# Splitting the generator's projection weights during the expert tiles and keeping the halves in DRAM

## The chip, the cores and the metric

The kernel is one program that runs on one core of a Trainium2 chip. Its time is device microseconds from start to end of the program, as a median of several executions. One further execution was taken with the hardware profiler; its trace is what the sections below read.

## What is computed

A two-layer decoder on x (32 sequences of 128 tokens, 256 features, written B, S and D in the kernel). Six stages follow each other, each adding to x. The two that matter here are the third and the fourth:

```python
# third stage: for each token the two best of 8 experts, weights by softmax of the two scores
u, v = x @ W1[e], x @ W2[e]
h = u * sigmoid(u) * v
out += (h @ W3[e]) * weights[..., e]
# fourth stage, on the normalized x
h_mean = mean(x, axis=1)                                  # one vector of 256 for each sequence
params = h_mean @ omega_proj_w.T + omega_proj_b           # 2016 numbers: the upper triangle of 64 x 64
omega = triangle(params) - triangle(params).T
G = I + omega + omega@omega/2 + omega@omega@omega/6
lie_out = (x[:, :, :64] @ G) @ omega_out_w.T + omega_out_b
out = rmsnorm(x + omega_mix * lie_out + vq_mix * vq_contribution, norm_w)
```

The weights of `params` (omega_proj_w) are the generator's projection weights. The host lays them out as a full 64 x 64 square for each of 256 features: 8192 f32 values on each of 128 partitions, 4 MB in all. The kernel multiplies with f16 pairs: a value times a power of two is kept as its f16 rounding (the high half) and the f16 of what is left (the low half), and a product is the sum of three f16 products.

## The kernel before, in words

**Order of the whole.** `decoder` calls six stage functions. Within one, each engine has its own instruction list, and semaphores order them; a block ends when every engine has reached its end. `give_back` then clears the stage's semaphores.

**The expert tiles (`expert_tiles`, from line 876).** The routing part before it sorts 2 x 4096 token choices into 39 tiles of 256 rows. For each tile GpSimd gathers the rows with two indirect DMAs (`gather`, L907, four tiles ahead) and scatters the results (`scatter`, L915). TensorE goes through: first half of the hidden columns (`up(n, 0)`), the rest of the tile before (`down(n-1, 1)`), the transposes of the next tile, `up(n, 1)`, `down(n, 0)`. ScalarE's and VectorE's lists are written out by hand in `step`: ScalarE does sigmoid, high half of h, result copy, high half of the next input, sigmoid, high half of h; VectorE does the gate (two operations), low half of h (L1038), low half of the next input (L1024), the gate again and the low half again. SyncE has nothing to do in this block.

**The generator stage (`lie_rotation`, from line 1689), its front.** SyncE issues, in this order, the 16 loads of expert results (eight groups of four sequences, two results for each token, 512 KB each), with the four quarters of the projection weights (`Wp`, 1 MB each, L1776) between them, then the constants and small weights, then the held weights of the next stage. VectorE adds the results to X (`add`, L2025: eight instructions to a group), takes statistics of two groups at a time (`stats`), GpSimd takes the root (`invert`, L1961), VectorE makes the shift (`negate`, L2049), ScalarE writes the normalized rows (`norm`, L1898), TensorE transposes the first 64 features (L1799) and sums the rows for the mean (L1803), ScalarE and VectorE keep the transposed rows as halves (`high` L1903, `low` L2055). VectorE's list is: add(2h), negate(h-1), add(2h+1), low(2h-2), stats(h), low(2h-1), for h = 1, 2, 3.

**The split before the change.** In ScalarE's list, `omega_piece` stands after the groups 2 and 3 (two quarters) and again after the groups 4 and 5 (two quarters); each is two activations over 2048 columns, one that scales `Wp` by 16 in place (L1908) and one that writes the high half (L1910). GpSimd's `omega_low` (L1966) makes the low half from the scaled weights and the high half: two quarters after `invert(2)`, two after `invert(3)`.

**What waits for it.** TensorE's `omega` (L1812: 64 rows of the square, six matmuls each, in seven runs with the code book's matmuls between them) waits for the four low quarters and for the mean's halves. `Wp` is afterwards used as scratch for the small results and for omega, which is why VectorE also waits for the low quarters ahead of the scratch's first use, and SyncE ahead of `shift_rows`.

Of the kernel before, what the change touches and what calls it, by code (L numbers as in the profile page):

```python
# [5 lines left out]
f16 = mybir.dt.float16  # L6
# [8 lines left out]
P = 128  # L15
# [552 lines left out]
def moe_swiglu(nc, sems, X, ident, power, A, ahead):  # L568

    SCALE = 256.0  # L570
    HID = HIDDEN
    HC = HID // P
    with ExitStack() as scope:
        c = Core(nc, scope, sems, "m_")
        owner = c.sb("owner", [P, TILES], i32)
        fetch, deliver = c.sb("fetch", [P, BLOCKS], u32), c.sb("deliver", [P, BLOCKS], u32)
        W1, W2 = ([c.sb(f"w{n}{t}", [P, E, DC, HID], f16) for t in range(2)] for n in (1, 2))
        W3 = [c.sb(f"w3{t}", [P, E, HC, D], f16) for t in range(2)]
        weights = [(A["split_w"][i, t], flat(w[t][:])) for i, w in enumerate((W1, W2, W3)) for t in range(2)]
        with ExitStack() as routing:  # L580
            dispatch(nc, Core(nc, routing, sems, "mr_"), X, ident, power, A, ahead, SCALE, weights, owner, fetch,
                     deliver)
        with ExitStack() as tiles:
            expert_tiles(nc, Core(nc, tiles, sems, "mt_"), ahead.area, ident, W1, W2, W3, SCALE, HC, owner, fetch,
                         deliver, A["token_rows"], A["expert_results"])

# [289 lines left out]
def expert_tiles(nc, c, area, ident, W1, W2, W3, SCALE, HC, owner, fetch, deliver, rows,  # L876
                 results):

# [18 lines left out]


    with nc.Block() as block:  # L899
        @block.gpsimd  # L900
        def _(pool):
# [78 lines left out]
        def _(act):  # L980
# [18 lines left out]
            def result(n, k, p, old):  # L999
# [3 lines left out]
                act.activation(yout[p][:, :, :], pY[:, :, :], ACT.Copy, scale=1.0 / SCALE).then_inc(y_copied, 1)  # L1003

            def step(n, k, p, age):
                sigmoid(n, 0, age == 0)
                hidden_high(n, 0, age == 0)
                if age > 0:
                    result(n - 1, k - 1 + p, 1 - p, not starts(n, 1) and not starts(n, 2))
                if not starts(n, TILES - 1):  # L1010
                    high(n + 1, 1 - p, age > 0)
                sigmoid(n, 1, age == 0)
                hidden_high(n, 1, age == 0)
            nc.scalar.preload_act_table(ACT.Sigmoid)
            high(0, 0, False)
            for n in range(TILES):
                step(n, n // 2, n % 2, min(n, 2))
            result(TILES - 1, (TILES - 1) // 2, 0, True)

        @block.vector  # L1020
        def _(dve):
# [19 lines left out]
            def step(n, k, p, age):  # L1041
# [4 lines left out]
                gate(n, 1, age == 0)  # L1046
                hidden_low(n, 1)
            low(0, 0)
            for n in range(TILES):
                step(n, n // 2, n % 2, min(n, 2))  # L1050


# [636 lines left out]
def lie_rotation(nc, sems, X, ident, power, A, ahead):  # L1689
# [5 lines left out]
    with ExitStack() as scope:  # L1695
# [24 lines left out]
        for n, rows, width in (("vq", B, LD), ("vsq", B, LD), ("csq", CODES, LD), ("bo2", B, D), ("vnorm", B, LD), ("cnorm", CODES, LD), ("vT", LD, B),  # L1720
# [35 lines left out]
            "consts_in w_in wp_in ones added1 added2 stat summed scaled ve rstd shifted xn turned high low meant kept "  # L1756
            "hm_high hm_low wp_scaled wp_high wp_low half_made norms step vq_projected vnorm cnorm both_turned turned_kept "
            "scores hot hot_turned hotT code_taken vqo vqo_turned vqoT vq_out shift16 shift_rows woo_mixed woo_high woo_low "
# [3 lines left out]
        def each(b0, n):  # L1762
            return slice(b0, b0 + n)

        with nc.Block() as block:
            @block.sync
            def _(sp):
                results = A["expert_results"][0:2 * B * S, :].rearrange("(k p b) d -> k p b d", k=2, b=B)
                piece = 0
                for g in range(NG):  # L1770
                    at = each(g * GB, GB)
                    sp.dma_start(XN[:, at, :], results[0][:, at, :]).then_inc(in1[g], 16)
                    sp.dma_start(R2[:, at, :], results[1][:, at, :]).then_inc(in2[g], 16)
                    if g in (1, 3, 4, 5):
                        columns = each(piece * WIDE, WIDE)
                        sp.dma_start(Wp[:, columns], flat(A["L1_attn_Wp"])[:, columns]).then_inc(s["wp_in"], 16)  # L1776
                        piece += 1
                sp.dma_start(mix[:, 0:1], A["L1_attn_omega_mix"].partition_broadcast(P)).then_inc(s["consts_in"], 16)
# [5 lines left out]
                for t, n in ((bvi, "L1_attn_vq_proj_in_b"), (bvo, "L1_attn_vq_proj_out_b"), (boo, "L1_attn_omega_out_b")):  # L1784
                    sp.dma_start(t[:, :], A[n].partition_broadcast(B)).then_inc(s["w_in"], 16)
                ahead.load(sp, "mqa")
                sp.wait_ge(s["shift16"], 2)
                sp.wait_ge(s["wp_low"], 4)
                for t in range(2):
# [3 lines left out]
            def _(pe):  # L1793
# [57 lines left out]
                last.then_inc(s["vq_projected"], 1)  # L1851
                pe.wait_ge(s["wp_low"], 4)
                pe.wait_ge(s["hm_low"], 1)
# [40 lines left out]
            def _(act):  # L1894
# [9 lines left out]

                def omega_piece(n):
                    columns = each(n * WIDE, WIDE)
                    act.wait_ge(s["wp_in"], 16 * 4)
                    act.activation(Wp[:, columns], Wp[:, columns], ACT.Copy, scale=PSCALE).then_inc(s["wp_scaled"], 1)  # L1908
                    act.wait_ge(s["wp_scaled"], n + 1)
                    act.activation(flat(Wp16[0][:])[:, columns], Wp[:, columns], ACT.Copy).then_inc(s["wp_high"], 1)  # L1910

                def G_high(h):
# [19 lines left out]
                for g in range(0, NG, 2):  # L1932
# [3 lines left out]
                    high(g + 1)  # L1936
                    if g == 2:
                        omega_piece(0)
                        omega_piece(1)
                    if g == 4:  # L1940
                        omega_piece(2)
                        omega_piece(3)
                act.wait_ge(s["meant"], 1)
# [13 lines left out]
            def _(pool):  # L1957
# [4 lines left out]

                def omega_low(n):
                    columns = each(n * WIDE, WIDE)
                    pool.wait_ge(s["wp_high"], n + 1)
                    pool.tensor_tensor(flat(Wp16[1][:])[:, columns], Wp[:, columns], flat(Wp16[0][:])[:, columns],  # L1966
                                       ALU.subtract).then_inc(s["wp_low"], 1)

                def root(g):
# [17 lines left out]
                invert(2)  # L1987
                omega_low(0)
                omega_low(1)
                invert(3)  # L1990
                omega_low(2)
                omega_low(3)
                pool.wait_ge(s["half_made"], 1)
# [11 lines left out]
            def _(dve):  # L2005
# [115 lines left out]
                for h in range(1, NG // 2):  # L2121
# [16 lines left out]
                   .then_inc(s["hm_low"], 1)  # L2138
                dve.wait_ge(s["wp_low"], 4)
                step(dve.tensor_scalar(v["bo2"][:, :], boo[:, :], mix[0:B, 0:1], None, ALU.mult))  # L2140
# [1033 lines left out]
def decoder(nc, A, out, stages):  # L3174
    with ExitStack() as whole:
# [15 lines left out]
        A["ctx_parts"] = nc.dram_tensor("ctx_parts", (2, NG, P, DC * GT), f16, kind="Internal").ap()  # L3191
        A["shares"] = nc.dram_tensor("shares", (NG // 2, 2 * GB * E, P), f32, kind="Internal").ap()
        A["m_bounce"] = nc.dram_tensor("m_bounce", (2, 2, D, GT), f16, kind="Internal").ap()
        ahead = Ahead(c, A, stages)
# [100 lines left out]
```

## Time and profile before

| | |
|---|---|
| median of three executions | 1752.41 us (1751.7 to 1754.59) |
| the profiled execution | 1740.78 us |
| its span, first to last instruction | 1739.1 us |
| TensorE busy over the span | 1300.8 us (75%) |
| VectorE, ScalarE, GpSimd busy | 62%, 47%, 43% |
| HBM read, written | 102.34 MB, 48.10 MB |

Spans and starts are counted from the first instruction. The stages lie at about 0 to 238 (attention), 238 to 579 (retention), 579 to 1015 (experts: routing up to 671, tiles up to 1008), 1015 to 1195 (generator), 1195 to 1456 (one-key attention) and 1456 to 1739 us (last stage). A busy share is an average over stages that have different limits, so the stage is read by itself. TensorE's granted clock is given as a share of 2.4 GHz: 0.50 is its lower level of 1.2 GHz throughout a stretch.

### The profile page before, as it was taken

What the parts mean: (1) busy time and instruction counts of PE and PEld (TensorE: products, weight loads), DVE (VectorE), ACT (ScalarE), POOL (GpSimd) and SP (SyncE); (2) the same over time, 40 slices, a digit from 0 to 9 for tenths busy, and PEclk for the clock granted to TensorE, in tenths of its full rate; (3) what the DMA queues carried; (4) which work ended last, traced back from release to release, by engine and by line L of the source; (5) the groups of instructions that cost most, each with busy time, mean ns of one, the idle gap of its engine ahead of it and who ended that gap; (6) DMA issues with size and microseconds to landing.
All of it is one profiled execution on the core that took longest, in us unless ns stands there. A gap on an engine that the chain in (4) does not pass through costs nothing. (4 is left out here: it accounts for less than half of the span.)

```text
span 1739.1 us, 33371 instructions
## 1 busy us (share of the span) xinstructions
PE 1300.8 (75%) x12335; PEld 997.5 (57%) x12335; DVE 1074.3 (62%) x2047; ACT 817.0 (47%) x1374; POOL 746.1 (43%) x639
## 2 busy tenths in 40 slices
PE   3766736788777336999999924894488886599997
PEld 2554523567665335999999924852356663366654
DVE  4778753776765556555555556456377863566664
ACT  2455443656654232444444416032176777466653
POOL 1333335989987202545554314033077788000000
PEclk9778857788886556999999965555698885699999
DMA  4433366665560531222222161004644230221330
GB/s 177 141 121 116 126 153 140 127 118 98 98 93 8 225 165 31 65 65 62 66 67 66 50 267 56 2 1 88 104 112 75 59 61 2 98 76 60 111 122 25
DMA packets 101678, 160.57 MB, mean 92 GB/s; under 512 B 14100, under 2 KB 70806, under 8 KB 99480
## 3 DMA queue, kind: packets, MB, share of 16 engines
q1 hardware_dynamic: 92504, 133.60, 29.7%
q0 software_dynamic: 8640, 24.65, 4.5%
q8 instruction: 101, 1.65, 0.4%
q14 instruction: 49, 0.40, 0.1%
q10 hardware_dynamic: 384, 0.26, 0.1%
HBM read 102.34 MB, written 48.10 MB: 87 GB/s over the span
## 5 line engine op out<-in xcount | busy, mean ns | idle before, releaser
L2670 POOL TENSOR_TENSOR q_pl<-q_ex,q_ph 128x512 f16<-128x512 f32 x128 | 147.2, 1161 | 42.1 <-ACT q_ph L2631 41.4
L1617 POOL TENSOR_TENSOR r_siml<-r_sim,r_simh 128x512 f16<-128x512 f32 x128 | 146.0, 1159 | 18.4 <-ACT r_simh L1519 18.1
L915 POOL DMA_INDIRECT expert_results<-mt_yout,m_deliver x78 | 77.4, 993 | 148.3 <-ACT mt_yout L1003 136.3
L2486 DVE TENSOR_REDUCE q_mx<-q_pS 128x4 f32<-128x512 f32 x128 | 86.6, 684 | 66.5 <-PE q_pS L2414 66.0
L1376 DVE TENSOR_TENSOR r_sim<-r_pS,r_causal 128x512 f32<-128x512 f32 x128 | 86.6, 682 | 57.3 <-PE r_pS L1290 53.5
L1519 ACT ACTIVATE r_simh<-r_sim 128x512 f16<-128x512 f32 x128 | 80.0, 628 | 87.2 <-DVE r_sim L1376 83.0
L948 PE MATMUL mt_pU<-mt_xh,m_w 128*128 128x256 f16 x624 | 116.2, 274 | 1.5 <-DVE mt_xl L1024 1.5
L907 POOL DMA_INDIRECT mt_xin<-token_rows,m_fetch x78 | 86.8, 1112 | 67.9 <-SPq L899 44.5
L948 PE MATMUL mt_pV<-mt_xh,m_w 128*128 128x256 f16 x624 | 115.3, 273 | 0.0
L959 PE MATMUL mt_pY<-m_w,mt_hh 128*128 x624 | 106.4, 273 | 1.0 <-DVE mt_hl L1038 1.0
L2882 PE MATMUL s_pY<-s_w,s_hh 128*128 128x256 f16 x576 | 101.1, 275 | 8.0 <-DVE s_hl L3104 6.6
L2625 ACT ACTIVATE q_ex<-q_pE 128x512 f32<-128x512 f32 x128 | 76.8, 600 | 61.0 <-PE q_pE L2435 41.0
L997 ACT ACTIVATE mt_hh<-ahead 128x512 f16<-128x512 f32 x78 | 49.2, 631 | 118.3 <-DVE ahead L1033 118.3
L2868 PE MATMUL s_pU<-s_XH,s_w 128*128 128x512 f16 x288 | 98.7, 385 | 0.0
L1030 DVE TENSOR_TENSOR ahead<-mt_pU,ahead 128x512 f32<-128x512 f32 x78 | 53.9, 691 | 66.9 <-ACT ahead L991 66.9
L2956 ACT ACTIVATE s_h<-s_pU,s_b 128x512 f32<-128x512 f32 x72 | 49.4, 686 | 82.7 <-PE s_pU L2868 82.5
L1038 DVE TENSOR_TENSOR mt_hl<-ahead,mt_hh 128x512 f16<-128x512 f32 x78 | 54.0, 692 | 54.3 <-ACT mt_hh L997 54.3
L3097 DVE TENSOR_TENSOR s_hc<-s_h,s_spread_share 128x512 f32<-128x512 f32 x64 | 44.2, 690 | 67.3 <-ACT s_h L2956 67.3
L948 PE MATMUL mt_pU<-mt_xl,m_w 128*128 128x256 f16 x312 | 85.6, 274 | 0.0
L948 PE MATMUL mt_pV<-mt_xl,m_w 128*128 128x256 f16 x312 | 85.2, 273 | 0.0
L959 PE MATMUL mt_pY<-m_w,mt_hl 128*128 x312 | 85.0, 273 | 0.0
L991 ACT ACTIVATE ahead<-mt_pU 128x512 f32<-128x512 f32 x78 | 46.6, 597 | 73.7 <-PE mt_pU L948 73.7
(511 smaller groups left out, 4124.5 us busy)
## 6 DMA issues: line engine op xcount, KB each, us to landing
s_spread_share<-shares SPq DMA_DIRECT2D x32, 512.0 KB, 6.2
a_pf<-in_L_ffn_W SPq DMA_DIRECT2D x24, 512.0 KB, 3.9
m_w<-split_w SPq DMA_DIRECT2D x6, 2048.0 KB, 22.5
split_w<-a_ph SPq DMA_DIRECT2D x24, 256.0 KB, 2.0
split_w<-a_pl SPq DMA_DIRECT2D x24, 256.0 KB, 2.7
r_kstack<-k_bounce SPq DMA_DIRECT2D x48, 128.0 KB, 4.7
r_qstack<-q_bounce SPq DMA_DIRECT2D x48, 128.0 KB, 6.0
q_Q<-m_bounce SPq DMA_DIRECT2D x24, 256.0 KB, 6.7
```

What stands on the lines that cost most here:

```text
L907: pool.indirect_dma_start(xin[n % INPUTS][:, a, :], None, rows[:, :], bass.IndirectOffsetOnAxis(ap=fetch[:, at:at + 1], axis=0))\
L915: pool.indirect_dma_start(results[:, :], bass.IndirectOffsetOnAxis(ap=deliver[:, at:at + 1], axis=0), yout[n % 2][:, a, :], None).then_inc ...
L948: last = pe.matmul(ps[half][:, j, :], W[x][:, e, dc, cols], (xh, xl)[y][p][:, dc, :], start=(m == 0), stop=(m == len(steps) - 1))
L959: last = pe.matmul(pY[:, a, :], (hh, hl)[x][half][:, j, a * P:(a + 1) * P], W3[y][:, e, half * HALF + j, :], start=half == 0 and j == 0 an ...
L1376: dve.tensor_tensor(sim[n % SIMS][:, :].rearrange("p (h t) -> p h t", t=S), pS[n % 2][:, :].rearrange("p (h t) -> p h t", t=S), repeat(tab ...
L1519: act.activation(simh[n % RING][:, :], sim[n % SIMS][:, :], ACT.Copy).then_inc(s["simh"], 1)
L1617: pool.tensor_tensor(siml[n % RING][:, :], sim[n % SIMS][:, :], simh[n % RING][:, :], ALU.subtract)\
L2486: dve.tensor_reduce(mx[:, at:at + UNIT], pS[n % 2][:, :, :], AX, ALU.max).then_inc(s["taken"], 1)
L2625: act.activation(ex[n % 3][:, :], pE[n % 2][:, :], ACT.Exp, scale=ATT).then_inc(s["exp"], 1)
L2670: pool.tensor_tensor(pl[n % RING][:, :], ex[n % 3][:, :], ph[n % RING][:, :], ALU.subtract)\
L2868: last = pe.matmul(pU[k % RING][:, :], W1[x][:, j, dc, :], (XH, XL)[y][:, dc, g * GT:(g + 1) * GT], start=(n == 0), stop=(n == len(steps) ...
L2882: last = pe.matmul(pY[:, b, :], (hh, hl)[x][k % RING][:, b * S:(b + 1) * S], W2[y][:, j, :], start=(j == 0 and n == 0 and b % 2 == 0), sto ...
```

## The change

The split moves out of the generator stage into the expert tiles. The weights are cut into eight pieces of 1024 columns. SyncE, idle in that block so far, loads a piece (512 KB f32) into one of two buffers and stores its two f16 halves (256 KB each) to a new DRAM tensor `omega_parts`. ScalarE makes the high half of a piece, in one activation that also scales, at the end of its list for the tiles 3, 7, ... 31. VectorE makes the low half one tile later (4, 8, ... 32), in one operation that scales and subtracts. In the generator stage the four loads of `Wp` and all of `omega_piece` and `omega_low` go; instead SyncE loads the two halves (2 MB each) after the small weights, and TensorE waits for these loads. Six semaphores come, three go.

```diff
@@ expert_tiles
+    OMEGA_SCALE, WIDE, PIECES_IN_FLIGHT, FIRST_PIECE, TILES_PER_PIECE = 16.0, 1024, 2, 3, 4
+    pieces = [slice(at, at + WIDE) for at in range(0, omega.shape[1], WIDE)]
+    pf = [c.sb(f"pf{i}", [P, WIDE]) for i in range(PIECES_IN_FLIGHT)]
+    ph, pl = ([c.sb(f"{n}{i}", [P, WIDE], f16) for i in range(PIECES_IN_FLIGHT)] for n in ("ph", "pl"))
+    def piece_due(n):
+        i, rest = divmod(n - FIRST_PIECE, TILES_PER_PIECE)
+        return i if rest == 0 and 0 <= i < len(pieces) else None
...
+        @block.sync
+        def _(sp):
+            for n in range(len(pieces) + PIECES_IN_FLIGHT):
+                if n >= PIECES_IN_FLIGHT:
+                    m = n - PIECES_IN_FLIGHT
+                    sp.wait_ge(piece_low, m + 1)
+                    for t, half in enumerate((ph, pl)):
+                        sp.dma_start(omega_parts[t][:, pieces[m]], half[m % PIECES_IN_FLIGHT][:, :])\
+                          .then_inc(piece_out[m % PIECES_IN_FLIGHT], 16)
+                if n < len(pieces):
+                    sp.dma_start(pf[n % PIECES_IN_FLIGHT][:, :], omega[:, pieces[n]])\
+                      .then_inc(piece_in[n % PIECES_IN_FLIGHT], 16)
...
+            def piece_upper(n):
+                i = n % PIECES_IN_FLIGHT
+                act.wait_ge(piece_in[i], 16 * (n // PIECES_IN_FLIGHT + 1))
+                if n >= PIECES_IN_FLIGHT:
+                    act.wait_ge(piece_out[i], 32 * (n // PIECES_IN_FLIGHT))
+                act.activation(ph[i][:, :], pf[i][:, :], ACT.Copy, scale=OMEGA_SCALE).then_inc(piece_high, 1)
...
                 step(n, n // 2, n % 2, min(n, 2))
+                if piece_due(n) is not None:
+                    piece_upper(piece_due(n))
...
+            def piece_lower(n):
+                i = n % PIECES_IN_FLIGHT
+                dve.wait_ge(piece_high, n + 1)
+                dve.scalar_tensor_tensor(pl[i][:, :], pf[i][:, :], OMEGA_SCALE, ph[i][:, :], ALU.mult, ALU.subtract)\
+                   .then_inc(piece_low, 1)
...
                 step(n, n // 2, n % 2, min(n, 2))
+                if piece_due(n - 1) is not None:
+                    piece_lower(piece_due(n - 1))
@@ lie_rotation
-                    if g in (1, 3, 4, 5):
-                        columns = each(piece * WIDE, WIDE)
-                        sp.dma_start(Wp[:, columns], flat(A["L1_attn_Wp"])[:, columns]).then_inc(s["wp_in"], 16)
-                        piece += 1
...
+                for t in range(2):
+                    sp.dma_start(flat(Wp16[t][:]), A["omega_parts"][t]).then_inc(s["wp_in"], 16)
                 ahead.load(sp, "mqa")
                 sp.wait_ge(s["shift16"], 2)
-                sp.wait_ge(s["wp_low"], 4)
...
-                pe.wait_ge(s["wp_low"], 4)
+                pe.wait_ge(s["wp_in"], 32)
...
-                def omega_piece(n):
-                    columns = each(n * WIDE, WIDE)
-                    act.wait_ge(s["wp_in"], 16 * 4)
-                    act.activation(Wp[:, columns], Wp[:, columns], ACT.Copy, scale=PSCALE).then_inc(s["wp_scaled"], 1)
-                    act.wait_ge(s["wp_scaled"], n + 1)
-                    act.activation(flat(Wp16[0][:])[:, columns], Wp[:, columns], ACT.Copy).then_inc(s["wp_high"], 1)
...
-                    if g == 2:
-                        omega_piece(0)
-                        omega_piece(1)
-                    if g == 4:
-                        omega_piece(2)
-                        omega_piece(3)
...
-                def omega_low(n):
-                    columns = each(n * WIDE, WIDE)
-                    pool.wait_ge(s["wp_high"], n + 1)
-                    pool.tensor_tensor(flat(Wp16[1][:])[:, columns], Wp[:, columns], flat(Wp16[0][:])[:, columns],
-                                       ALU.subtract).then_inc(s["wp_low"], 1)
...
                 invert(2)
-                omega_low(0)
-                omega_low(1)
                 invert(3)
-                omega_low(2)
-                omega_low(3)
...
-                dve.wait_ge(s["wp_low"], 4)
```

## Rows read from the trace of the kernel before

**Rows 1.** Windows: stretch, length, busy time of the five engines, PEclk, DMA share, GB/s.

```profile
800.00:900.00 100.00, 100.00 (x919) 90.18 (x917) 58.25 (x85) 41.57 (x74) 51.19 (x49) 1.00 0.21 65
1015.00:1196.00 181.00, 117.76 (x910) 90.47 (x910) 110.39 (x234) 55.50 (x125) 52.91 (x36) 0.50 0.20 75
1196.00:1456.00 260.00, 193.97 (x2574) 137.33 (x2574) 178.18 (x392) 154.51 (x293) 162.19 (x154) 0.79 0.44 84
```

**Rows 2.** Timeline of PE, generator stage: start, length, line, idle before and its releaser.

```profile
1083.84 1.06 PE L1799 MATMUL l_pair<-ident,l_XN 128*64 128x128 f32 x4 [6.92 <-ACT l_XN L1898]
...
1093.15 7.86 PE L1812 MATMUL l_pair<-l_hm,l_Wp 128*64 128x32 f16 x144
```

**Rows 3.** Timeline of ACT in the generator stage.

```profile
1066.42 4.04 ACT L1898 ACTIVATE l_XN<-X,l_shift,l_rstd 128x256 f32<-128x256 f32 x8 [5.40 <-DVE l_shift L2049]
...
1079.91 1.91 ACT L1910 ACTIVATE l_Wp<-l_Wp 128x2048 f16<-128x2048 f32 x1
1081.73 4.02 ACT L1898 ACTIVATE l_XN<-X,l_shift,l_rstd 128x256 f32<-128x256 f32 x8
...
1092.25 0.22 ACT L1944 ACTIVATE l_hm<-l_pair 128x64 f32<-128x64 f32 x1 [2.62 <-PE l_pair L1803]
```

**Rows 4.** Timeline of DVE in the generator stage.

```profile
1042.06 1.65 DVE L2025 SCALAR_TENSOR_TENSOR X<-l_XN,part,X 128x256 f32<-128x256 f32 x4
...
1045.41 0.16 DVE L2049 SCALAR_TENSOR_TENSOR l_shift<-l_mean,l_rstd 128x8 f32<-128x8 f32 x1
...
1054.91 1.66 DVE L2025 SCALAR_TENSOR_TENSOR X<-l_XN,part,X 128x256 f32<-128x256 f32 x4
1057.02 9.29 DVE L2025 SCALAR_TENSOR_TENSOR X<-l_R,part,X 128x256 f32<-128x256 f32 x4 [0.46 <-DVE X L2025]
1066.23 0.15 DVE L2049 SCALAR_TENSOR_TENSOR l_shift<-l_mean,l_rstd 128x8 f32<-128x8 f32 x1
...
1076.94 0.17 DVE L2049 SCALAR_TENSOR_TENSOR l_shift<-l_mean,l_rstd 128x8 f32<-128x8 f32 x1 [1.16 <-POOL l_rstd L1961]
```

**Rows 5.** Timeline of POOL in the generator stage.

```profile
1057.35 8.28 POOL L1966 TENSOR_TENSOR l_Wp<-l_Wp 128x2048 f16<-128x2048 f32 x2 [1.06 <-ACT l_Wp L1910]
```

**Rows 6.** Windows around the loads of the stage, columns as in rows 1.

```profile
1030.00:1052.00 22.00, 12.61 (x61) 12.23 (x62) 19.02 (x55) 9.63 (x19) 3.04 (x2) 0.50 0.96 362
1052.00:1087.00 35.00, 15.64 (x77) 15.04 (x75) 23.19 (x51) 24.94 (x28) 19.82 (x6) 0.50 0.00 1
```

**Rows 7.** One tile of the expert loop on ACT and DVE, timelines.

```profile
811.55 0.63 ACT L997 ACTIVATE mt_hh<-ahead 128x512 f16<-128x512 f32 x1 [1.50 <-DVE ahead L1033]
813.38 0.60 ACT L991 ACTIVATE ahead<-mt_pU 128x512 f32<-128x512 f32 x1 [1.20 <-PE mt_pU L948]
...
812.21 0.69 DVE L1038 TENSOR_TENSOR mt_hl<-ahead,mt_hh 128x512 f16<-128x512 f32 x1 [0.70 <-ACT mt_hh L997]
814.01 0.69 DVE L1030 TENSOR_TENSOR ahead<-mt_pU,ahead 128x512 f32<-128x512 f32 x1 [1.10 <-ACT ahead L991]
```

**Rows 8.** The same tile on PE (its next down starts) and POOL, timelines.

```profile
814.49 0.38 PE L959 MATMUL mt_pY<-m_w,mt_hh 128*128 x2
...
816.87 0.99 POOL L915 DMA_INDIRECT expert_results<-mt_yout,m_deliver  x1 [3.13 <-ACT mt_yout L1003]
```

**Rows 9.** Prices: lines and tiles asked by name, ns min/median/max.

```profile
L493 ACT ACTIVATE a_ph<-a_pf x24: 1056/1057/1058, 38.7 to 230.9; 128x1024 f16<-128x1024 f32 x24
...
L1038 DVE TENSOR_TENSOR mt_hl<-ahead,mt_hh x78: 691/692/694, 684.7 to 1002.6; 128x512 f16<-128x512 f32 x78
...
L785 DVE TENSOR_TENSOR mr_xl<-mr_turn,mr_xh x8: 1216/1224/1225, 591.5 to 629.9; 128x1024 f16<-128x1024 f32 x8
...
L2025 DVE SCALAR_TENSOR_TENSOR X<-l_R,part,X x32: 473/479/4295, 1020.6 to 1069.3; 128x256 f32<-128x256 f32 x32
```

**Rows 10.** Start of the tiles: POOL and PE timelines.

```profile
672.05 1.04 POOL L907 DMA_INDIRECT mt_xin<-token_rows,m_fetch  x1 [44.46 <-SPq L899]
...
676.23 1.11 PE L935 MATMUL mt_turn<-ident,mt_xin 128*128 128x128 f32 x4 [7.38 <-DMA mt_xin<-token_rows,m_fetch]
```

More of the change, by code:

```diff
@@ L584, in moe_swiglu @@
             expert_tiles(nc, Core(nc, tiles, sems, "mt_"), ahead.area, ident, W1, W2, W3, SCALE, HC, owner, fetch,
-                         deliver, A["token_rows"], A["expert_results"])
+                         deliver, A["token_rows"], A["expert_results"], flat(A["L1_attn_Wp"]), A["omega_parts"])
 def dispatch(nc, r, X, ident, power, A, ahead, SCALE, weights, owner, fetch, deliver):
@@ L876, in expert_tiles @@
 def expert_tiles(nc, c, area, ident, W1, W2, W3, SCALE, HC, owner, fetch, deliver, rows,
-                 results):
+                 results, omega, omega_parts):
     HALF = HC // 2
@@ L896, in expert_tiles @@
                           "y_copied".split())
-    with nc.Block() as block:
+    OMEGA_SCALE, WIDE, PIECES_IN_FLIGHT, FIRST_PIECE, TILES_PER_PIECE = 16.0, 1024, 2, 3, 4
+    pieces = [slice(at, at + WIDE) for at in range(0, omega.shape[1], WIDE)]
+    pf = [c.sb(f"pf{i}", [P, WIDE]) for i in range(PIECES_IN_FLIGHT)]
+    ph, pl = ([c.sb(f"{n}{i}", [P, WIDE], f16) for i in range(PIECES_IN_FLIGHT)] for n in ("ph", "pl"))
+    piece_in, piece_out = ([c.sem(f"{n}{i}") for i in range(PIECES_IN_FLIGHT)] for n in ("piece_in", "piece_out"))
+    piece_high, piece_low = c.sem("piece_high"), c.sem("piece_low")
+    def piece_due(n):
+        i, rest = divmod(n - FIRST_PIECE, TILES_PER_PIECE)
+        return i if rest == 0 and 0 <= i < len(pieces) else None
+    with nc.Block() as block:
+        @block.sync
[10 more added lines that the diff above has]
+                      .then_inc(piece_in[n % PIECES_IN_FLIGHT], 16)
+            for i in range(PIECES_IN_FLIGHT):
+                sp.wait_ge(piece_out[i], 32 * len(range(i, len(pieces), PIECES_IN_FLIGHT)))
         @block.gpsimd
@@ L1756, in lie_rotation @@
             "consts_in w_in wp_in ones added1 added2 stat summed scaled ve rstd shifted xn turned high low meant kept "
-            "hm_high hm_low wp_scaled wp_high wp_low half_made norms step vq_projected vnorm cnorm both_turned turned_kept "
+            "hm_high hm_low half_made norms step vq_projected vnorm cnorm both_turned turned_kept "
             "scores hot hot_turned hotT code_taken vqo vqo_turned vqoT vq_out shift16 shift_rows woo_mixed woo_high woo_low "
@@ L1768, in _ @@
                 results = A["expert_results"][0:2 * B * S, :].rearrange("(k p b) d -> k p b d", k=2, b=B)
-                piece = 0
                 for g in range(NG):
@@ L3192, in decoder @@
         A["shares"] = nc.dram_tensor("shares", (NG // 2, 2 * GB * E, P), f32, kind="Internal").ap()
+        A["omega_parts"] = nc.dram_tensor("omega_parts", (2, P, DC * LD * LD), f16, kind="Internal").ap()
         A["m_bounce"] = nc.dram_tensor("m_bounce", (2, 2, D, GT), f16, kind="Internal").ap()
```

## Prediction

> **What bounds the kernel now.** I read the windows by stage first, then the timelines engine by engine inside the two stages that the change touches. The expert tiles are bound by TensorE: in the middle of the loop it is busy 100.00 of 100 us at a granted clock of 1.00, while VectorE is busy 58 and ScalarE 42 [rows 1]. The generator stage is bound by nothing for long: TensorE is busy 118 of 181 us, VectorE 110, ScalarE 56, GpSimd 53, the clock is 0.50 (1.2 GHz) throughout [rows 1]. So it is a chain through all of them, and what shortens a link of the chain shortens the stage. In its front half the links are: results added on VectorE, statistics, root on GpSimd, shift, normalized rows on ScalarE, transposes and mean on TensorE. TensorE's list is idle 6.92 us ahead of the last transposes, for ScalarE's rows, and `omega` starts at 1093.15 [rows 2]. The reader should see there that `omega` doesn't wait for the split: it starts 0.9 us after the mean's copy at 1092.25 [rows 3], which itself ended a wait for TensorE. The split costs time earlier, where its instructions stand in front of the chain's.
>
> **What the removal gives.** Two links of that chain are longer than their work.
>
> First, on VectorE. Four adds of one half take 1.65 us, and from the start of an undisturbed group's adds to the shift behind them 1045.41 - 1042.06 = 3.35 us pass. In the next round that stretch is 1066.23 - 1054.91 = 11.32 us, because the four adds from 1057.02 take 9.29 us [rows 4]; single adds of this line take 479 ns in the median and 4295 at most [rows 9]. GpSimd's two `omega_low` run from 1057.35 for 8.28 us [rows 5]: the adds have been executing, not waiting for a load, and only beside these two. Removal: 11.32 - 3.35 = 7.97 us. The Trainium skill ("SBUF — State Buffer", engine ports) says that a GpSimd operation and a VectorE operation with two SBUF inputs exclude each other for a whole instruction on a shared pair of ports; the trace agrees, each of the two longest adds being about as long as one of the two GpSimd operations.
>
> Second, on ScalarE. The last shift is ready at 1076.94 [rows 4], but ScalarE still has `omega_piece` quarters until 1079.91 + 1.91, and the last normalized rows start at 1081.73, with no idle time before them. The round before had started 0.19 us behind its shift (1066.42 against 1066.23) [rows 3, 4]. Without the pieces the last round starts at 1076.94 + 0.19 = 1077.13: 4.60 us earlier.
>
> Both lie in series, so the last rows start at 1081.73 - 7.97 - 4.60 = 1069.16, and all behind them keeps its distance: **-12.6 us** at `omega`'s start, about 1080.6. What is late next? The round before: its rows would start at 1066.42 - 7.97 = 1058.45, TensorE begins 1083.84 - 1081.73 = 2.1 us behind a round's rows and needs 1092.25 - 1083.84 = 8.4 us for its transposes and sums [rows 2, 3], so it is done by about 1069, before the last rows exist; it doesn't bind. The loads: TensorE now waits for 4 MB of halves instead of work on 4 MB of f32, the stage moves the same bytes, and all of them are in by 1052, after which the DMA moves 1 GB/s [rows 6]; 28 us of slack against 1080.6. The results come earlier if anything, as nothing stands between them in SyncE's list, but VectorE waits for a load only once, at its first add, whose load was first in the list already: 0. The held weights of the next stage are loaded behind 4 MB more and needed only after 1196: 0. The waits for the low quarters on VectorE and SyncE were long fulfilled: 0.
>
> **What the tiles pay.** Eight pieces are added. On ScalarE a piece costs 1.06 us, the price of the same shape from SBUF [rows 9]; it stands behind the second high half of h, which ends at 812.18, and ahead of a sigmoid that waits 1.20 us for TensorE until 813.38 [rows 7]. It ends at about 813.2: it fits. On VectorE a piece is taken at 1.22 us, the price of a 1024-wide subtraction [rows 9]. It stands behind the low half that ends at 812.90, and the gate behind it starts at 814.01 after 1.10 us idle [rows 7]. So the gate may be 0.1 to 0.2 us late. Who waits for that? Not TensorE's next `down` at 814.49, since its low half was finished at 812.90, before the piece [rows 7, 8]; the late gate's low half, one half-tile on, has the same kind of margin, 814.49 - 812.90 = 1.6 us. The loop forgives this 8 times: 0. The other end: none of it is hidden, 8 x (1.06 + 1.22) = 18.2 us. I take 0, as the gaps are in the very places where the pieces stand.
>
> The pieces' low halves have two SBUF inputs too, and GpSimd issues indirect DMAs all through the loop. L1038 is an operation of this kind beside them, and 78 of it lie between 691 and 694 ns [rows 9], so VectorE isn't held. By the port rule of the Trainium skill ("SBUF — State Buffer") the descriptors of a gather could be held for a piece's length instead. GpSimd is idle 3.13 us in a tile [rows 8] and gathers four tiles ahead; 8 x 1.22 = 9.8 us is the price if that were no cover. I take 0.
>
> SyncE gets eight loads and sixteen stores. It has nothing queued behind them in that block, and the DMA share of the loop is 0.21 [rows 1]: 8 MB of traffic in 300 us don't fill it. One place is tight: the first two pieces are issued as the block opens, together with the first gather, for which TensorE waits from 672.05 to 676.23 with an empty list [rows 10]. Their 1 MB at the 362 GB/s of rows 6 is 2.9 us of transfer. Bounds 0 and 2.9; part of it passes while the gather is still being issued, so I take **+1.0**. Three more semaphores on balance and a DRAM tensor: 0, within 0.3 either way, at the stage's borders.
>
> **Sum.** -12.6 + 1.0 = -11.6 us. The profiled execution goes from 1740.78 to 1729.2. The median of the runs is 11.6 us above that execution; no view shows where, so I leave it as it is and take the change off the median: 1752.41 - 11.6 = **1740.8 us**.
>
> **The rivals.**
> - The forecast, with its own bounds (0 to 2.9 at the tiles' start, 0.3 at the borders): 1739.5 to 1743. Chance 0.74.
> - The clock of the later stages moves. They start 12 us earlier against whatever the chip looks at; the one-key stage runs at 0.79 with 194 us of matmul [rows 1], and a mean clock 0.01 off is some 2.5 us. For it: the clock there isn't at one level. Against: the gaps of that stage come from its own waits, and move along. Two hundredths either way on the forecast: 1736 to 1746. Chance 0.09.
> - Only one stall goes, because something else holds the adds or the last rows (a late load, the high halves). 1752.41 - 4.6 + 1.0 = 1748.8, or -8.0 + 1.0 = 1745.4. Against it: each stall has its cause beside it in the same microseconds. Chance 0.07.
> - The change doesn't do what it says, and `omega` waits for its halves. It needs a landing after 1093 to take all, where the same bytes were in by 1052: 1752 to 1753. Chance 0.02.
> - GpSimd is held by the pieces: -11.6 + 9.8, 1750.6. Chance 0.04.
> - Slower: the pieces lie on TensorE's path. It decides when a piece delays a low half beyond the 1.6 us of margin, for instance if ScalarE or VectorE waits for a piece's other half or for its store; then 8 x 2.28 - 11.6 = +6.6, 1759.0. Against it: each piece is ordered one tile ahead of its reader, and a load lies 30 us ahead of its use. Chance 0.04.
>
> **How the numbers follow.** 0.2% is 3.5 us, about what a measurement of this kernel can tell from no change. Faster by more: 0.74 + 0.09 + 0.07 = 0.90. Within: 0.02 + 0.04 = 0.06. Slower: 0.04. The range takes the forecast, the clock's spread and most of the half gains: 1736 to 1748, leaving about 0.12 outside.
>
> **What would show it.** In the profile of after: no add of L2025's line over 0.5 us; the last two rounds of normalized rows 10.7 us apart (1076.94 - 1066.23) with ScalarE idle before the last; `omega` some 12 us earlier from the stage's first load; the stretch from there to the end of the stage unchanged in length; the tile loop still without TensorE idle, its length from first transpose to last result unchanged within 0.5 us; TensorE's wait for the first gather up to 2.9 us longer. Wrong would be: TensorE waiting in tiles 3 to 32 for a low half, `omega` waiting for a load, or later stages of another length.

## The result and the profile after

The changed kernel took 1744.47 us (median of 6, 1742.03 to 1747.51) beside 1753.18 us for the kernel before (median of 6, 1751.7 to 1756.7): ratio 0.9949, 95% interval 0.9935 to 0.9963, so 6.5 to 11.4 us faster. In two later comparisons the same pair gave 1731.83 against 1742.47 us (0.9933, 0.9913 to 0.9953) and 1730.48 against 1741.62 us (0.9927, 0.9906 to 0.9948). One of the twelve executions of e6 below took 5820 us; its median is 1740.45 us with it and 1739.68 us without.

The page of after, its first lines:

```profile
span 1742.6 us, 33404 instructions
## 1 busy us (share of the span) xinstructions
PE 1303.0 (75%) x12335; PEld 995.5 (57%) x12335; DVE 1072.3 (62%) x2055; ACT 806.2 (46%) x1374; POOL 725.8 (42%) x635
...
PEclk9888857788886556999999975555788886699999
```

The span of this profile is 3.5 us longer than that of before (1739.1), though the timed medians say the opposite. That contradiction is the first thing to read. A table by stage, from the starts of the first or last instruction of the groups concerned (us; omega is TensorE's first matmul on the generator's weights, a result is ScalarE's copy of a tile's output):

| profile | first gather to transposes | to first result | first to last result | to first load of the generator stage | to omega | to the end |
|---|---|---|---|---|---|---|
| before | 4.2 | 15.3 | 313.4 | 10.3 | 77.9 | 645.9 |
| after | 4.8 | 16.2 | 326.9 | 10.4 | 65.7 | 645.5 |

The generator stage lost 12.2 us up to omega, what stands behind it kept its length, and the tile loop (first to last result) was 13.5 us longer. A longer loop, with TensorE waiting for low halves in it, is what the prediction had named as a sign of being wrong. The experiments below had to say whether that belongs to the pieces.

Generator stage, the rows that answer to [rows 2 to 5]. The timelines of after for ScalarE (ACT), VectorE (DVE), SyncE's queue (SPq) and TensorE (PE), in this order:

```profile
1074.87 4.04 ACT L1937 ACTIVATE l_XN<-X,l_shift,l_rstd 128x256 f32<-128x256 f32 x8 [4.92 <-DVE l_shift L2065]
...
1085.60 4.04 ACT L1937 ACTIVATE l_XN<-X,l_shift,l_rstd 128x256 f32<-128x256 f32 x8 [2.81 <-DVE l_shift L2065]
...
1096.14 0.22 ACT L1970 ACTIVATE l_hm<-l_pair 128x64 f32<-128x64 f32 x1 [2.61 <-PE l_pair L1842]
```

```profile
1071.33 1.65 DVE L2041 SCALAR_TENSOR_TENSOR X<-l_XN,part,X 128x256 f32<-128x256 f32 x4
1073.09 1.67 DVE L2041 SCALAR_TENSOR_TENSOR X<-l_R,part,X 128x256 f32<-128x256 f32 x4
1074.67 0.16 DVE L2065 SCALAR_TENSOR_TENSOR l_shift<-l_mean,l_rstd 128x8 f32<-128x8 f32 x1
...
1085.40 0.17 DVE L2065 SCALAR_TENSOR_TENSOR l_shift<-l_mean,l_rstd 128x8 f32<-128x8 f32 x1 [1.16 <-POOL l_rstd L1987]
```

```profile
1031.37 0.32 SPq L1814 DMA_DIRECT2D l_XN<-expert_results  x1
...
1051.78 1.13 SPq L1825 DMA_DIRECT2D l_Wp<-omega_parts  x2
```

```profile
1087.73 1.06 PE L1838 MATMUL l_pair<-ident,l_XN 128*64 128x128 f32 x4 [2.36 <-ACT l_XN L1937]
...
1097.04 7.86 PE L1851 MATMUL l_pair<-l_hm,l_Wp 128*64 128x32 f16 x144
```

The reader sees the four adds back at 1.67 us, where they took 9.29; from the adds' start to the shift 3.34 us, where it was 11.32 [rows 4]; the last normalized rows 0.20 us behind their shift with ScalarE idle before them, where they were 4.8 us behind [rows 3]; and TensorE idle 2.36 us ahead of the last transposes, where it was 6.92 [rows 2].

The tile loop of after, the longest waits of PE from 676 to 1022 us and then ACT's from 700 to 1020 us (us in total, how many, longest us):

```profile
PE mt_pY L985 <- DVE mt_hl L1073: 11.3, 17, 1.0
PE mt_turn L961 <- DMA mt_xin<-token_rows,m_fetch: 8.0, 1, 8.0
```

```profile
ACT ahead L1017 <- remote: 46.1, 18, 2.9
ACT ahead L1017 <- PE mt_pU L974: 20.0, 18, 2.3
```

TensorE waited 17 times for a low half; in the profile of before once, at the very end (the same view from 660 to 1025 us):

```profile
PE mt_pY L959 <- DVE mt_hl L1038: 1.0, 1, 1.0
```

The other 16 waits of after stand in about every second tile from tile 5 to tile 36 and take 10.3 of the 13.5 us. The halves were late because ScalarE's sigmoids were, and those waited for TensorE's signal; one such wait stands at tile 2, before the first piece is touched:

```profile
700.91 0.60 ACT L1017 ACTIVATE ahead<-mt_pU 128x512 f32<-128x512 f32 x1 [2.32 <-PE mt_pU L974]
...
710.23 0.60 ACT L1017 ACTIVATE ahead<-mt_pU 128x512 f32<-128x512 f32 x1 [2.94 <-remote]
...
716.53 1.04 ACT L1036 ACTIVATE mt_ph<-mt_pf 128x1024 f16<-128x1024 f32 x1
```

The sigmoid at 710.23 needs the product whose last matmul TensorE's records put here:

```profile
707.77 0.27 PE L974 MATMUL mt_pU<-mt_xh,m_w 128*128 128x256 f16 x1
```

That is 2.2 us from the recorded end to the sigmoid's start. In the profile of before it is 0.04 us in nearly all of the 78 half tiles and never more than 0.1; in this one it is 0.4 to 3.0 us in 70 of the 78, from tile 2 to tile 36, and 0.04 us again in the last two tiles. The ends of matmuls are modelled, so the records don't say whether the signals came late or the matmuls themselves did.

### The profile page after: what moved, and what is told of

Same layout as the page of the kernel before. It is cut to its first block and busy times, and to the rows that moved or that the text cites. A ratio compares the mean times of both kernels' runs of the same rounds, so it can differ in the third digit from the quotient of the medians.

```text
span 1742.6 us, 33404 instructions
## 1 busy us (share of the span) xinstructions
PE 1303.0 (75%) x12335; PEld 995.5 (57%) x12335; DVE 1072.3 (62%) x2055; ACT 806.2 (46%) x1374; POOL 725.8 (42%) x635
## 5 line engine op out<-in xcount | busy, mean ns | idle before, releaser
L2501 DVE TENSOR_REDUCE q_mx<-q_pS 128x4 f32<-128x512 f32 x128 | 86.7, 685 | 66.0 <-PE q_pS L2429 65.4
L985 PE MATMUL mt_pY<-m_w,mt_hh 128*128 x624 | 106.6, 272 | 11.4 <-DVE mt_hl L1073 11.3
L933 POOL DMA_INDIRECT mt_xin<-token_rows,m_fetch x78 | 82.3, 1055 | 68.2 <-POOLq L632 44.7
L2646 ACT ACTIVATE q_ph<-q_ex 128x512 f16<-128x512 f32 x128 | 80.5, 629 | 0.0
```

The source lines that it names most:

```text
L933: pool.indirect_dma_start(xin[n % INPUTS][:, a, :], None, rows[:, :], bass.IndirectOffsetOnAxis(ap=fetch[:, at:at + 1], axis=0))\
L985: last = pe.matmul(pY[:, a, :], (hh, hl)[x][half][:, j, a * P:(a + 1) * P], W3[y][:, e, half * HALF + j, :], start=half == 0 and j == 0 an ...
L2501: dve.tensor_reduce(mx[:, at:at + UNIT], pS[n % 2][:, :, :], AX, ALU.max).then_inc(s["taken"], 1)
L2646: act.activation(ph[n % RING][:, :], ex[n % 3][:, :], ACT.Copy).then_inc(s["ph"], 1)
```

## The experiments

Theory A: the change gains 12.2 us in the generator stage and costs about 1 us at the tiles' start, and the long loop has nothing to do with it. Theory B: the pieces make the loop long.

**The kernel before, again.** No edit.

> The kernel before, unchanged, profiled a second time. In the first profile its tile loop has no idle TensorE (transposes at 676.23 to last result 1005) and the execution took 1740.8 us, 12 us under its own timed median; in the profile of the changed kernel the loop is 14 us longer and TensorE waits 17 times for a low half. Theory A (the loop has a slower mode that has nothing to do with the pieces): this profile shows the longer loop, about 343 us, with such waits, and a time of 1751 to 1755. Theory B (the pieces make the loop longer): the loop is 328.7 us again. Timed against itself: ratio 1.000.

Measured: 1740.48 us, ratio to itself 0.9995 (0.9979 to 1.0011). From first transposes to last result 328.7 us passed (313.4 from the first result), and TensorE waited once for a half. So Theory B's number came out, and Theory A's long loop and 1751 to 1755 us did not. But the timed median of before was now 1742, not 1753: the level of the measurement had moved by 11 us, and this run alone can't tell the theories apart; the next three, timed beside it, can.

**The changed kernel, again.** No edit.

> The changed kernel, unchanged, a second time, beside the others on one chip. Theory A: 12.2 us gained in the generator stage, 0.7 to 3 lost in the tiles, 1741 to 1744.5 against 1753; ratio 0.993 to 0.9955. Theory B: the same ratio, but 14 us lost in the tiles and something else in the kernel before that explains its 1753.

Measured: 1731.83 us, ratio 0.9933 (0.9913 to 0.9953). Loop 313.4 us, omega 65.5 us behind the first load. The same program with the same eight pieces ran the loop at before's length: the pieces by themselves don't make the loop long, and Theory B is out as written. That they have a part in a long loop when it comes isn't excluded by this. A piece in this profile, DVE and its neighbours:

```profile
729.12 0.69 DVE L1073 TENSOR_TENSOR mt_hl<-ahead,mt_hh 128x512 f16<-128x512 f32 x1 [0.70 <-ACT mt_hh L1023]
729.73 1.22 DVE L1086 SCALAR_TENSOR_TENSOR mt_pl<-mt_pf,mt_ph 128x1024 f16<-128x1024 f32 x1
730.91 0.69 DVE L1065 TENSOR_TENSOR ahead<-mt_pU,ahead 128x512 f32<-128x512 f32 x1
...
739.21 0.69 DVE L1065 TENSOR_TENSOR ahead<-mt_pU,ahead 128x512 f32<-128x512 f32 x1 [1.10 <-ACT ahead L1017]
```

The gate behind the piece starts at 730.91, the one of the next tile at 739.21, 8.30 us later, which is the tile's length: the piece has filled the 1.10 us gap and delayed nothing by more than can be read.

**Only the tiles' part.** `lie_rotation` is that of before; `omega_parts` is written and not read.

> Only the tiles' part of the change: the eight pieces are split and stored during the tiles, but nobody reads them; the generator stage is that of before. This is the price of the pieces alone. Theory A as I priced it: +1.0 us at the tiles' start, nothing in the loop: +0.7 to +1.5 us. Theory A with a smaller margin in the longer loop: +3 to +4 us. Theory B: +14 us.

Measured: 1742.00 us, ratio 0.9996 (0.9983 to 1.0009), that is -3.0 to +1.6 us. Loop 313.4 us, first gather to transposes 5.4 us against 4.2. The price of the pieces is below what the timing resolves; +14 and +3 us are excluded.

**Only the generator's part.** The tiles are those of before, and the halves come from another tensor of the same shape, so the generator computes with other weights:

```diff
-                    sp.dma_start(flat(Wp16[t][:]), A["omega_parts"][t]).then_inc(s["wp_in"], 16)
+                    sp.dma_start(flat(Wp16[t][:]), A["split_w"][t, 1]).then_inc(s["wp_in"], 16)
```

> Only the generator's part: the loads of f32 weights, the scaling, the high and the low halves go, and the two halves are loaded from DRAM, but from a tensor of other f16 values of the same shape (low halves of the experts' weights), so that the tiles need no pieces; the generator's weights are therefore other values. The tile loop is that of before. Theory A: the whole gain without its price, -12.2 us, ratio 0.9930. Theory B gives the same here; if the timed gain is below 10 us, the two stalls cost less in timed executions than in the profiled one.

Measured: 1729.84 us, ratio 0.9928 (0.9910 to 0.9947), 12.6 us faster; omega 65.8 us behind the first load. This is the gain without its price, in timed executions: 12.2 us were expected, of either theory.

**The first stall alone.** In the kernel before:

```diff
+                    columns = slice(columns.start, columns.start + 64)
                     pool.tensor_tensor(flat(Wp16[1][:])[:, columns], Wp[:, columns], flat(Wp16[0][:])[:, columns],
...
-                            last = pe.matmul(p1[j * 2 // LD][0:LD, at:at + B], Wp16[w][:, dc, j, :], hm16[x][:, dc, :],
+                            last = pe.matmul(p1[j * 2 // LD][0:LD, at:at + B], Wp16[0][:, dc, j, :], hm16[x][:, dc, :],
```

> The kernel before with GpSimd's four low-half operations cut to 64 of their 2048 columns, and the low halves' matmuls reading the high halves instead, so the generator's product is computed with other weights; ScalarE's part of the split is whole. It takes away the first stall alone (VectorE's adds beside GpSimd). If the two stalls are what I say and add up: -8.0 us, no add of X over 0.5 us, and the last normalized rows start 4.6 us behind their shift, as before. If the gain hangs on the pieces' place on ScalarE instead: about 0. If the adds were slow because of the loads or of ScalarE: the 4.3 us adds stay.

Measured: 1737.39 us, ratio 0.9974 (0.9961 to 0.9987), 2.3 to 6.8 us faster, and omega 72.4 us behind the first load against 77.9: 5.5 us, not 8.0. The mechanism holds: the longest add took 529 ns where it was 4295. The size doesn't. DVE and ACT of this run:

```profile
1057.87 1.72 DVE L2026 SCALAR_TENSOR_TENSOR X<-l_R,part,X 128x256 f32<-128x256 f32 x4 [0.46 <-DVE X L2026]
1059.51 0.15 DVE L2050 SCALAR_TENSOR_TENSOR l_shift<-l_mean,l_rstd 128x8 f32<-128x8 f32 x1
```

```profile
1059.96 1.91 ACT L1910 ACTIVATE l_Wp<-l_Wp 128x2048 f16<-128x2048 f32 x1
1061.77 4.02 ACT L1898 ACTIVATE l_XN<-X,l_shift,l_rstd 128x256 f32<-128x256 f32 x8
```

The third shift is ready at 1059.51, but ScalarE still has the first two quarters of its own split until 1061.8, and the rows start 2.3 us behind the shift, where it was 0.2. In the kernel before, this wait lay hidden under the held adds. That is 2.1 of the 2.5 us that are missing. Nearly all of the rest is VectorE's 0.46 us of idle time between the adds, which is in before too and not in after; no row says what it waits for. The gain of one cause was cut short by the other.

**The second stall alone.** In the kernel before:

```diff
                     act.wait_ge(s["wp_in"], 16 * 4)
+                    columns = slice(columns.start, columns.start + 64)
                     act.activation(Wp[:, columns], Wp[:, columns], ACT.Copy, scale=PSCALE).then_inc(s["wp_scaled"], 1)
...
-                    pool.tensor_tensor(flat(Wp16[1][:])[:, columns], Wp[:, columns], flat(Wp16[0][:])[:, columns],
+                    pool.tensor_tensor(flat(Wp16[1][:])[:, columns], Wp[:, columns], Wp[:, columns],
```

> The complement: the kernel before with ScalarE's eight operations of the split cut to 64 columns, GpSimd's four low-half operations whole in length (they subtract the weights from themselves, and the generator's matmuls read these zeros, so its product is nothing). It takes away the second stall alone. Expected: the last normalized rows start 0.2 us behind their shift, -4.6 us; VectorE's adds are still held for 8 us by GpSimd. If both stalls were one: -12 or 0.

Measured: 1740.45 us, ratio 0.9990 (0.9977 to 1.0003), a difference that is not clear of noise; omega 75.5 us behind the first load: 2.3 us gained (77.90 less 75.55), not 4.6. So this gain is read from one profile. POOL and DVE show why it is small:

```profile
1078.17 7.28 POOL L1967 TENSOR_TENSOR l_Wp<-l_Wp 128x2048 f16<-128x2048 f32 x2
```

```profile
1059.78 7.82 DVE L2026 SCALAR_TENSOR_TENSOR X<-l_R,part,X 128x256 f32<-128x256 f32 x4 [0.46 <-DVE X L2026]
...
1078.24 3.55 DVE L2050 SCALAR_TENSOR_TENSOR l_shift<-l_mean,l_rstd 128x8 f32<-128x8 f32 x1 [1.16 <-POOL l_rstd L1962]
```

With ScalarE's part short, GpSimd begins its last two quarters at once, and now they meet the last shift: an operation on 128x8 values that takes 0.17 us elsewhere took 3.55. The last rows start as soon as the shift ends, as expected, but the shift ends 3.4 us late: the wait on ScalarE was replaced by one beside GpSimd's subtraction. So the two stalls are two causes (each edit took away its own), worth 5.5 and 2.3 us one at a time and 12.2 together.

**The first pieces later.** In the changed kernel:

```diff
+            sp.wait_ge(turned, 2)
             for n in range(len(pieces) + PIECES_IN_FLIGHT):
```

> The changed kernel with SyncE waiting for the transposes of the second tile before it loads the first piece. In four profiles the wait from the first gather's issue to the first transposes is 4.15 to 4.24 us without pieces and 4.84 to 5.36 with them, and the first tile (first transposes to first result) takes 15.2 to 15.4 without and 16.2 to 16.6 with them. If the first two pieces' loads do this: 4.2 and 15.3 again, 1.6 us less than the changed kernel, -12.2 us against before (ratio 0.9930). If the loads only share the blame with chance (the clock's rise): 4.2 but still 16.2, -11.2 us.

Measured: 1730.00 us, ratio 0.9936 (0.9913 to 0.9958), not to be told from the changed kernel. From gather to transposes it took 4.2 us again: that part is the pieces' doing. From there to the first result it still took 16.5 us. It also took 16.6 in e6, which has no pieces, and 15.2 to 15.4 in the five other profiles without them. What this part follows is TensorE's granted clock. Windows from the first transposes to the first result, columns as in rows 1, of before, e6 and e7:

```profile
676.23:691.57 15.34, 13.84 (x107) 11.61 (x108) 6.72 (x10) 4.56 (x9) 4.43 (x5) 0.81 0.18 52
677.43:694.01 16.58, 15.08 (x106) 12.34 (x107) 6.77 (x10) 4.67 (x8) 4.36 (x5) 0.75 0.16 48
676.38:692.87 16.49, 14.99 (x107) 12.34 (x108) 6.73 (x10) 4.67 (x9) 4.41 (x5) 0.75 0.36 112
```

TensorE is idle for 1.50 us in each; only its busy time grows. The mean clock of this stretch is 0.81 in all five profiles with 15.2 to 15.4 us and 0.74 to 0.76 in all eight others: the clock goes from 0.50 to 1.00 5.6 to 6.0 us behind the first transposes in the five and 7.7 to 8.6 us behind them in the eight. All seven profiles of kernels with pieces are among the eight, and one of the six without. Why the rise comes later isn't shown.

**How much room the loop has.** In the changed kernel, with two more f16 tiles `extra`:

```diff
+                for t in range(2):
+                    dve.scalar_tensor_tensor(extra[t][:, :], pf[i][:, :], OMEGA_SCALE, ph[i][:, :], ALU.mult, ALU.subtract)
                 dve.scalar_tensor_tensor(pl[i][:, :], pf[i][:, :], OMEGA_SCALE, ph[i][:, :], ALU.mult, ALU.subtract)\
                    .then_inc(piece_low, 1)
```

> The changed kernel with each piece's low half computed three times on VectorE (3.5 us instead of 1.2 in one place, eight times). It asks how much room the loop has there. By the timeline of before the gap is 1.1 us and TensorE's next need of a half made behind it comes 2.0 us late at the earliest (low half finished 816.83, down at 818.86): 3.5 - 1.1 - 2.0 = 0.4 us each, +2 to +4 us in the loop over the changed kernel. If the room were the gap alone: 8 x 2.3 = +18 us. If VectorE's work there is free at any length: 0. GpSimd's gathers beside the piece should be longer by up to a piece's length, since they share the ports, without TensorE waiting for one.

Measured: 1734.08 us, ratio 0.9953 (0.9936 to 0.9970); the loop took 316.1 us against 313.4, +2.7 for eight pieces, 0.34 each, close to the 0.4 worked out. DVE of this run: the piece now lasts from 723.56 to 727.05.

```profile
723.56 2.35 DVE L1088 SCALAR_TENSOR_TENSOR mt_extra<-mt_pf,mt_ph 128x1024 f16<-128x1024 f32 x2
725.83 1.22 DVE L1089 SCALAR_TENSOR_TENSOR mt_pl<-mt_pf,mt_ph 128x1024 f16<-128x1024 f32 x1
726.96 0.69 DVE L1066 TENSOR_TENSOR ahead<-mt_pU,ahead 128x512 f32<-128x512 f32 x1
```

GpSimd's gathers beside it were not longer than in the loop of before (1295 ns at most, for both): that part of the expectation missed. Seven of the eight began 0.37 us ahead of the long piece and one 0.72, and GpSimd's next operation 2.7 us behind its end.

**The same, twice instead of three times.** `range(1)` in place of `range(2)`.

> The changed kernel with each piece's low half computed twice on VectorE (2.35 us in one place). Tripled, it made the loop (first to last result) 316.1 us against 313.4. With a gap of 1.1 us and room of 2.0 behind it, 2.35 - 1.1 is inside the room: 313.4, no cost. If the tripled piece's 2.7 us were paid in proportion to the added length, 314.8.

Measured: loop 313.4 us, no cost; 1732.15 us, ratio 0.9947 (0.9927 to 0.9967), of four executions. The cost sets in between 2.35 and 3.5 us, and the piece as it is, at 1.22, is well inside.

**Both kernels a third time.** No edits.

> The kernel before once more, for its profile on whatever chip this is. From first to last result the tile loop took 313.3 to 313.4 us in eight profiles, with pieces and without, and 326.9 us in the first profile of the changed kernel alone. If the long loop belongs to a chip or an execution, this shows 313.4, or 327 with a time some 12 us above 1742; if it needs the pieces, it is never seen here: 313.4 always.

> The changed kernel once more beside it. If the long loop belongs to the chip, this one and the kernel before show the same loop; if to the pieces in some executions, this one may show 327 alone. In the generator stage: first load to the generator's first matmul 65.5 us as in the two profiles so far, against 77.8 to 78.2 without the change.

Measured: before 1739.96 (ratio to itself 0.9997), loop 313.4, omega at 78.1; changed 1730.48 us, ratio 0.9927 (0.9906 to 0.9948), loop 313.4, omega at 65.6. The long loop didn't come back in either. The eleven runs were on three chips (e1 to e4, e5 to e8, e9 to e11), with no long loop on any of them; which one timed the first pair is not on record.

The profiles together, in the columns of the table above (kernels with pieces from the start of the tiles: e2, e3, e8, e9, e11):

| profile | gather to transposes | to first result | first to last result | to omega | to the end |
|---|---|---|---|---|---|
| e1_before_again | 4.2 | 15.2 | 313.4 | 78.1 | 642.2 |
| e10_before_third | 4.2 | 15.4 | 313.4 | 78.1 | 645.6 |
| e3_tiles_only | 5.4 | 16.5 | 313.4 | 77.9 | 646.6 |
| e4_generator_only | 4.1 | 15.2 | 313.4 | 65.8 | 640.6 |
| e5_short_low | 4.2 | 15.3 | 313.4 | 72.4 | 644.4 |
| e6_short_high | 4.3 | 16.6 | 313.4 | 75.5 | 649.3 |
| e2_after_again | 4.8 | 16.3 | 313.4 | 65.5 | 645.1 |
| e11_after_third | 5.0 | 16.7 | 313.4 | 65.6 | 645.5 |
| e7_load_after_tile1 | 4.2 | 16.5 | 313.4 | 65.5 | 645.1 |
| e9_low_twice | 5.2 | 16.6 | 313.4 | 65.4 | 642.5 |
| e8_low_thrice | 5.1 | 16.6 | 316.1 | 65.5 | 643.2 |

The last column is very nearly the same work in all of them and spreads over 8.7 us. What stands ahead of the table varies too: the first gather starts between 671.8 and 678.6 us. That is the noise against which 12 us has to be seen, and why the columns in the middle say more than the totals.

## Why the prediction held, step by step

- **The first stall.** Put at 7.97 us; in after the stretch took 3.34 instead of 11.32, 7.98 less. The cause, GpSimd's subtraction beside adds with two SBUF inputs, is shown by e5, where it alone was made short. The port rule that the prediction took from the Trainium skill ("SBUF — State Buffer", "SBUF: two separate sides") fits e6 as well: a 0.17 us operation took 3.55 beside GpSimd's.
- **The second stall.** Put at 4.60; the last rows start 0.20 us behind their shift, and the last two rounds are 10.73 us apart, as worked out (10.7). e6, where ScalarE's part alone was short, shows the cause: there the last rows start at 1081.83, as soon as their shift ends (1081.79).
- **Their sum.** Put at 12.6; up to omega 12.2 in the first pair (77.9 to 65.7), 12.2 to 12.7 between any of the three profiles of before and the three of after. 0.3 of what the first pair lacks is the first load, which VectorE waited for 3.5 us instead of 3.2. What was next in line, the round before and the loads, was late in neither: TensorE had 2.36 us of idle time left, and the halves, issued by 1052.5 with at most 18.1 us to landing, were in by 1070.6, 26 us ahead of omega; I had said 28.
- **The loop.** Put at 0 within bounds up to 18.2. It took 313.4 us with pieces and without, except for e8's long ones and the one profile of 326.9. In that profile TensorE did wait for low halves, in tiles 5 to 36, which the prediction had named as a sign of being wrong; but ScalarE's late sigmoids begin in tile 2, ahead of the first piece, and e2 and e11 ran the same pieces, e9 longer ones, in 313.4 us. My 1.6 us of room was the smaller of two numbers; e8 and e9 put the edge between 2.35 and 3.5 us of length, and 1.1 + 2.0 = 3.1 fits, where 1.1 + 1.6 = 2.7 would have made e8 cost 6 us.
- **The tiles' start.** Put at +1.0 between 0 and 2.9. Gather to transposes: 4.8 to 5.4 us in six profiles with early pieces, 4.1 to 4.3 in six profiles without and 4.2 in e7, so 0.6 to 1.2. Another 0.9 to 1.3 us up to the first result goes with the clock, which rises later in the first tile (mean 0.74 to 0.76 instead of 0.81); the prediction has no term for it. e6 and e7 have it as well without early pieces, so whether the change brings it stays open.
- **The size.** -11.6 us forecast. Measured -8.7 (6.5 to 11.4), -10.6, -11.1; the ratio of the forecast, 0.9934, lies 0.0001 outside the first interval and inside the other two. By the stages, omega's gain less the two columns at the tiles' start, the three pairs of profiles give 10.7, 11.0 and 10.4. The median of 1744.47 us lies in the stated range, but 3.7 us above the forecast and outside the bounds that the forecast itself was given (1739.5 to 1743); 0.8 of that is the level of before, 1753.18 for 1752.41.
- **The level.** I could not place the 11.6 us between the profiled execution of before and its median. Later medians of before were 1742, near that profile. One cause of this size has been seen: the loop of 326.9 instead of 313.4 us, in one profile of the changed kernel, taken where before was timed at 1753. That it was this in the kernel before as well is not shown, as no profile of before was taken with a long loop. What speaks for it is arithmetic alone: the profiled execution of after, 1744.28 us, lies in the middle of its six, and less 13.5 us it is 1730.8, where the changed kernel was timed later; 1753.2 less 13.5 is 1739.7. That the absolute time fell into the range therefore owes something to both kernels having been at the same level in the first comparison.
- **The rivals.** The pieces on TensorE's path (+6.6) are excluded by the loop's length. GpSimd held (9.8) is excluded as a price: gathers were held, as the last section shows, but TensorE waited for none behind the first. The clock of the later stages did not move with the change: in the one-key stage it is 0.79 to 0.83 in the six profiles where omega starts late and 0.79 to 0.82 in the seven where it starts early, and the stretch behind omega is 642.2 to 649.3 us in the six and 640.6 to 645.5 in the seven. The clock doesn't order these lengths either: it was 0.82 in the longest and 0.80 in the shortest. That `omega` waits for its halves is excluded by their landing. The rival "only one stall goes" was priced wrongly: I took each stall off by itself, 8.0 and 4.6, where alone they bring 5.5 and 2.3, because each hides part of the other. That did not hurt the forecast, since both went.

## What to carry to other kernels

Work moved off a chain is worth the whole of the stalls that it made, and those are found in the durations (adds of 4.3 us among adds of 0.48) as much as in the waits. Where two causes hold the same chain, the price of removing one is read by following the other through the new times, not by subtraction. Room for added work is a gap plus the distance to the next reader's need; here 1.1 + 2.0 us, with the first cost seen between 2.35 and 3.5 us.

## What was not expected of the hardware

A GpSimd operation on two SBUF inputs held even a VectorE operation on 8 columns for its own length (3.55 us instead of 0.17). GpSimd's indirect DMA did not hold VectorE at all, but was itself held. In the profile of after the second gather begins 0.33 us behind each of the eight pieces, and there it takes 1.73 to 1.74 us where 1.29 was the most before. POOL of after, beside the piece that VectorE began at 725.35:

```profile
725.68 1.73 POOL L933 DMA_INDIRECT mt_xin<-token_rows,m_fetch  x1 [0.30 <-issue]
```

POOL of e2, where the gather began ahead of the piece at 729.73, within the low half of h at 729.12:

```profile
729.35 1.29 POOL L933 DMA_INDIRECT mt_xin<-token_rows,m_fetch  x1 [0.30 <-issue]
```

Both end 0.84 us behind the end of the VectorE operation in which they began (726.57 and 729.81). So it is in all thirteen profiles: the gathers that begin within a low half of h or a piece, both with two SBUF inputs, end 0.83 to 0.87 us behind that operation, and those that begin within the gate, which has one input in PSUM, take 0.96 to 0.99 us.

And the tile loop, though its TensorE is granted the full clock (1.00) throughout and idle in the records for less than 4% of it, once ran 4% longer, with the sigmoids starting up to 3.0 us behind the recorded ends of their matmuls, where it is 0.1 us at most in the ten other profiles without a lengthened piece. It was seen in one profile of thirteen, and what makes it stays open.
